# New order tables for a software-pipelined two-layer mixer kernel, and its expert weights fetched by SyncE

## The reference

```python
x = L0_attn_x                                   # [16, 512, 128] float32
xn = _layernorm(x)
s = _L0_attn_ref(xn, ...)                       # full softmax attention, 16 heads of 8
g = _silu(_L0_ffn_ref(xn, W1, W2, Wg, bg))      # top-1 of 8 experts, 128 -> 512 -> 128, gelu
x = x + s * g
xn = _layernorm(x)
s = _L1_attn_ref(xn, ...)                       # windows of 32 tokens + 64 pooled latents, gated
g = _silu(_L1_ffn_ref(xn, ...))                 # two local-attention layers (window 64, rotary,
                                                # 8 heads of 64), each with a gated feed-forward
x = x + s * g

# the expert layer
logits = xf @ Wg + bg
one_hot = jax.nn.one_hot(jnp.argmax(logits, axis=-1), e)
h = gelu(einsum('td,edh->eth', xf, W1)); y = einsum('eth,ehd->etd', h, W2)
out = einsum('etd,te->td', y, one_hot)

# one of the two layers inside _L1_ffn_ref
qkv = shift_token(x) @ wqkv; q, k = rotary_xpos(l2norm(q) * qs, l2norm(k) * ksc)
x = x + local_attention(q, k, v) @ wo
h = layernorm(shift_token(x)) * lg + lb
a, g = split(h @ w1 + b1); x = x + (a * gelu(g)) @ w2 + b2
```

## Time and profile before

| what | value |
|---|---|
| time of three runs | 3394.94, 3395.32, 3401.74 us, median 3395.32 |
| the profiled execution | 3426.32 us, of which 3424.5 us from first to last instruction |
| mean granted TensorE clock | 0.963 of full speed |
| PE busy | 3140.8 us, 92% |
| DVE busy | 2438.6 us, 71% |
| ACT busy | 2337.1 us, 68% |
| POOL busy | 1273.1 us, 37% |
| DMA | 133.97 MB, mean 39 GB/s |

### The profile page before, as it was taken

The page is one execution under the profiler, slowest core; times in us unless marked ns, Lnnn a source line. Parts: engine busy times, 40 slices in busy tenths (PEclk is TensorE's granted clock), DMA queues, the critical chain, the costliest instruction groups (busy, mean ns, idle before and its releaser), DMA issues.

```text
span 3424.5 us, 83892 instructions
## 1 busy us (share of the span) xinstructions
PE 3140.8 (92%) x34202; PEld 1900.2 (55%) x34202; DVE 2438.6 (71%) x4967; ACT 2337.1 (68%) x4800; POOL 1273.1 (37%) x817
## 2 busy tenths in 40 slices
PE   5799799999999999999999999999999999999976
PEld 5268545556564646555565646464555656464644
DVE  6621486868687877868686868778686868787643
ACT  4342277777767776777777677867777777777754
POOL 1146034433333343444333334334443333343343
PEclk8699799999999999999999999999999999999988
DMA  5346200101011111001010111110010101111000
GB/s 152 96 122 175 54 22 23 36 17 41 24 31 34 31 31 34 25 27 31 17 41 24 31 34 31 31 34 25 28 31 17 41 24 34 31 31 31 5 13 4
DMA packets 128412, 133.97 MB, mean 39 GB/s; under 512 B 18004, under 2 KB 110910, under 8 KB 128030
## 3 DMA queue, kind: packets, MB, share of 16 engines
q1 hardware_dynamic: 117872, 98.84, 11.1%
q0 software_dynamic: 10160, 29.76, 3.1%
HBM read 80.98 MB, written 30.28 MB: 32 GB/s over the span
## 4 chain that ended last, share of the span: by engine, by line
PE 53%; DVE 15%; ACT 10%; POOL 7%; issue 4%; DMA 0%; POOLq 0%; ACTq 0%; DVEq 0%
PE bank L2015 5%; PE bank L725 5%; PE bank L1453 4%; PE bank L2059 4%; PE bank L1466 4%; PE bank L2001 3%; DVE turn_f L2188 3%; PE bank L1437 3%; DVE nmax_a L1577 3%; PE bank L1982 2%; POOL turn_f L1930 2%; PE bank L1957 2%; PE bank L1991 2%; POOL y_a L1499 2%; PE bank L2065 2%
## 5 line engine op out<-in xcount | busy, mean ns | idle before, releaser
L1522 ACT ACTIVATE prob_a<-bank 128x512 f32<-128x512 f32 x1024 | 559.2, 603 | 172.0 <-PE bank L1466 165.8
L1577 DVE TENSOR_REDUCE nmax_a<-bank 128x1 f32<-128x512 f32 x768 | 499.4, 685 | 71.4 <-PE bank L1437 64.2
L1924 POOL TENSOR_TENSOR rn<-ss,minus_half 128x16 f32<-128x16 f32 x128 | 392.4, 3065 | 283.7 <-DVE ss L2183 281.8
L1947 POOL TENSOR_TENSOR rs_f<-rs_f,minus_half 128x4 f32<-128x4 f32 x32 | 32.5, 1017 | 1127.5 <-DVE rs_f L1317 1127.5
L1930 POOL TENSOR_TENSOR turn_f<-turn_f 128x512 f32<-128x512 f32 x256 | 324.8, 1289 | 169.9 <-DVE turn_f L2188 169.9
L1466 PE MATMUL bank<-Qst_a,Kst_a 74*128 74x512 bf16 x1024 | 373.4, 389 | 8.4 <-DVE nmax_a L1577 3.1
L2077 ACT ACTIVATE area<-bank 128x512 f32<-128x512 f32 x640 | 347.2, 597 | 49.6 <-PE bank L2015 41.2
L2188 DVE TENSOR_TENSOR turn_f<-area,rotf 128x1024 f32<-128x1024 f32 x256 | 306.2, 1219 | 7.2 <-POOL area L1934 6.2
L1437 PE MATMUL bank<-Kst_a,Qst_a 72*128 72x512 bf16 x768 | 302.3, 394 | 7.0 <-DMA Kst_a<-dk_a 2.4
L1453 PE MATMUL bank<-prob_a,V_a 128*9 128x512 f32 x2048 | 275.4, 610 | 26.1 <-ACT prob_a L1522 25.8
L1934 POOL TENSOR_TENSOR area<-turn_f,rn 128x1024 f32<-128x1024 f32 x128 | 254.6, 1989 | 18.6 <-POOL turn_f L1930 0.4
(11 more groups left out here) (303 smaller groups left out, 7009.6 us busy)
## 6 DMA issues: line engine op xcount, KB each, us to landing
Qst_a<-dq_a SPq DMA_DIRECT2D x192, 96.0 KB
Kst_a<-dk_a SPq DMA_DIRECT2D x192, 96.0 KB
dq_a<-prob_a SPq DMA_DIRECT2D x80, 128.0 KB
dk_a<-prob_a SPq DMA_DIRECT2D x48, 128.0 KB
ys_d<-otok_f SPq DMA_DIRECT2D x39, 128.0 KB
x_a<-in_x_in SPq DMA_DIRECT2D x16, 256.0 KB, 2.9
xn_b<-xn_n SPq DMA_DIRECT2D x16, 256.0 KB, 2.5
x_b<-x_a SPq DMA_DIRECT2D x16, 256.0 KB, 2.9
```

The lines of the kernel that those rows point to most:

```text
L1522: nc.scalar.activation(dst, bk.full(act, product)[0:rows, :], func, **kw).then_inc(a_emptied["act"], 1)
L1577: nc.vector.tensor_reduce(out=nmax_a[:, g, t, j:j + 1], in_=bk.full(dve, f)[:], op=ALU.max, axis=AX.X, negate=True).then_inc(emptied, 1)
L1924: nc.gpsimd.tensor_tensor(rn[:, t % 2], ss[:, t % 2], minus_half[:], ALU.pow).then_inc(f_root, 1)
```

## The change

Three things change.

1. All tables are replaced: `STEP`, the tables of `TIMES` and `OPEN`, and the strings of `SEATS`. The streams and their slots stay the same except for the one below. `STEP` falls from 180.102 to 178.7555.
2. `weights(j)` moves from GpSimd's stream of the opening to a new stream of SyncE, `weights_sync`. For each of the 39 blocks SyncE reads one number of `m_offs` into a register and issues a plain DMA of 128 rows of `W12`, 512 KB.
3. GpSimd no longer waits for the weights' semaphores at the opening's end, nor resets them; SyncE waits for them there.

Line numbers of the changed kernel are larger by 3 from line 924 on, and smaller by 1 between about lines 861 and 877 (the gathers L894 are L908 there).

```diff
-STEP = 180.102
+STEP = 178.7555
...
-                     (3.3175, 9.27123, 35.56572, 49.41184, 63.61356)),
+                     (4.90434, 7.96273, 8.60039, 27.32943, 51.26716)),
+            "weights": ((60, 164.1, 169, 173.9, 178.8, 183.7, 188.6, 193.5, 198.4, 203.3, 208.2, 213.1, 218,
...
+        def weights_sync(sp):
+            def weights(j):
+                first_row = sp.value_load(m_offs[0:1, j:j + 1], min_val=0, max_val=(NX - 1) * P)
+                sp.dma_start(w_ring[j % WS], W12[bass.ds(first_row, P), :]).then_inc(m_w[j % WS], 16)
+
+            yield 60
+            sp.wait_ge(m_pos, 5)
+            for j in range(WS_EARLY):
+                weights(j)
+            for j in range(WS_EARLY, NBLK):
+                yield block_slot(j - XS) + 1
+                if j == WS_EARLY:
+                    sp.wait_ge(m_sorted, 16 * 4)
+                if j >= WS:
+                    sp.wait_ge(m_y, j - WS + 1)
+                weights(j)
+            yield block_slot(NBLK) + 9.5
+            for i in range(WS):
+                sp.wait_ge(m_w[i], 16 * len(range(i, NBLK, WS)))
...
-            def weights(j):
-                nc.gpsimd.indirect_dma_start(
-                    out=w_ring[j % WS], out_offset=None, in_=W12,
-                    in_offset=bass.IndirectOffsetOnAxis(ap=m_offs[:, j:j + 1], axis=0)).then_inc(m_w[j % WS], 16)
...
-                if j >= WS_EARLY:
-                    yield block_slot(j - XS) + 1
-                    if j >= WS:
-                        pool.wait_ge(m_y, j - WS + 1)
-                    weights(j)
             yield block_slot(NBLK) + 9
-            for i in range(WS):
-                pool.wait_ge(m_w[i], 16 * len(range(i, NBLK, WS)))
```

More of the change, by code:

```diff
@@ L69 @@
             "head": ((0, 9.5, 12, 17, 29.6),
-                     (3.3175, 9.27123, 35.56572, 49.41184, 63.61356)),
+                     (4.90434, 7.96273, 8.60039, 27.32943, 51.26716)),
+            "weights": ((60, 164.1, 169, 173.9, 178.8, 183.7, 188.6, 193.5, 198.4, 203.3, 208.2, 213.1, 218,
[7 rows of a table added]
             "a": ((14, 34, 36, 56, 59, 83),
-                  (59.33356, 69.68172, 78.86345, 143.92706, 168.55117, 171.7043))},
[1 row of a table added]
         "gpsimd": {
-            "open": ((15, 18, 21, 24, 27, 30, 33, 36, 60, 147.4, 152.3, 157.2, 162.1, 164.1, 167, 169, 171.9,
[18 rows of a table removed]
+            "open": ((15, 18, 21, 24, 27, 30, 33, 36, 147.4, 152.3, 157.2, 162.1, 167, 171.9, 176.8, 181.7,
+                      186.6, 191.5, 196.4, 201.3, 206.2, 211.1, 216, 220.9, 225.8, 230.7, 235.6, 240.5, 245.4,
+                      250.3, 255.2, 260.1, 265, 269.9, 274.8, 279.7, 284.6, 289.5, 294.4, 299.3, 304.2, 309.1,
+                      314, 318.9, 323.8, 328.7, 333.6, 368.1),
+                     (-729.096, -545.2831, -221.3447, -180.39589, -180.39389, -139.05282, -36.43666, 27.16759,
+                      317.98284, 319.70985, 353.57071, 403.3216, 556.39821, 591.40663, 591.40863, 632.65447,
+                      757.3734, 995.69333, 1026.89636, 1214.81975, 1216.69564, 1351.08384, 1463.7214,
+                      1486.61817, 1514.8511, 1572.56744, 1574.60451, 1579.50739, 1603.88541, 1603.88741,
+                      1645.15018, 1645.15218, 1645.15418, 1647.91192, 1647.91392, 1647.91592, 1647.91792,
+                      1647.91992, 1647.92192, 1647.92392, 1647.92592, 1647.92792, 1647.92992, 1647.93192,
+                      1647.93392, 1647.93592, 1760.56987, 3896.46718)),
             "head": ((1, 2),
-                     (-196.74222, -195.74222))},
+                     (94.66748, 95.66748))},
         "tensor": {
@@ L252 @@
             "b": ((1.3, 2.3),
-                  (51.04818, 52.04818)),
+                  (-0.06161, 0.93839)),
             "head": ((0, 9.5, 12, 17, 29.6),
-                     (-13.55572, 22.639, 40.46466, 46.27433, 58.46796)),
+                     (-13.57442, -10.67782, 21.78004, 34.99895, 45.90457)),
             "f": ((0, 8.1, 14.2),
-                  (-41.95577, -35.8369, -30.77378)),
+                  (-129.22774, -124.54517, -67.15646)),
             "a": ((14, 34, 36, 56, 59, 83),
-                  (-103.46081, -103.45881, -97.04039, -61.756, -57.1256, -35.48245)),
+                  (-137.1201, -124.26509, -119.78701, -106.34444, -91.74503, -67.28961)),
             "finish": ((14.7, 15.7),
-                       (-48.84137, -47.84137))},
+                       (-67.57821, -66.57821))},
         "gpsimd": {
             "gate": ((0, 1),
-                     (-57.76785, -56.76785)),
+                     (-53.54468, -52.54468)),
             "b": ((0.5, 1.5),
-                  (-18.78003, -17.78003)),
+                  (-44.93433, -43.93433)),
             "head": ((1, 2),
[1 row of a table removed]
[1 row of a table added]
             "f": ((5, 6.5, 10.4, 11.9, 15.8, 17.3, 21.2, 22.7, 47, 70, 71.5, 75.4, 76.9, 80.8, 82.3, 86.2, 87.7),
[2 rows of a table removed]
[2 rows of a table added]
             "feed": ((6.8, 7.8),
-                     (-116.27669, -115.27669))},
+                     (-110.06641, -109.06641))},
         "tensor": {
@@ L378 @@
                    96.4, 97.6, 98.8, 100, 101.2, 102.4, 104.6, 108),
[10 rows of a table removed]
[10 rows of a table added]
             "feed": ((6.175, 8.3, 8.55, 9.05, 9.55),
-                     (-124.31877, -112.73997, -108.16469, -107.46893, -106.33904)),
+                     (-116.73057, -106.30141, -103.55657, -103.17137, -100.22011)),
             "finish": ((11.2, 12.2),
-                       (-98.06906, -97.06906))},
+                       (-63.94697, -62.94697))},
         "vector": {
             "gate": ((113, 113.2, 113.4),
[1 row of a table removed]
[1 row of a table added]
             "b": ((0, 0.2, 0.5, 1.5, 2.6, 3, 3.2, 3.5, 5.1, 5.2, 5.3, 5.35, 7.1, 7.2, 7.3, 7.35, 9.1, 9.2, 9.3,
@@ L425 @@
                    98.4, 99.6, 100.8, 102, 103.5, 105, 111),
[10 rows of a table removed]
[10 rows of a table added]
             "feed": ((6.55, 6.8, 7.1, 8.8, 9.3, 9.8, 10.725),
-                     (-117.34283, -116.7413, -114.69475, -107.49325, -106.47296, -104.13016, -98.61513)),
+                     (-112.76509, -111.65438, -110.77237, -103.08967, -101.79345, -99.4833, -77.78949)),
             "finish": ((13.2, 13.4, 13.6),
-                       (-85.7543, -81.99587, -49.48497))}}
+                       (-58.22573, -55.4072, -53.6288))}}
 SEATS = {
-    "a": ("254203542054321042053241510303423411324514003545035030402552035230451350243510500531031024"
-          "3120353102545202400520502353505"),
-    "b": "050234504111500034533154315435550000",
-    "head": "01221103413415325431",
-    "f": ("102451231531052304031214125341452150324254414530140041321435103131243505035235421312352412"
-          "4311012042240200"),
-    "feed": "033045214"}
+    "a": ("154203542054415324103240512302323013124514003554035030102035022530543105243150130531013001"
+          "4532011520531051023103150350342"),
+    "b": "550243503111500034533453305032530452",
+    "head": "32010321541515105430",
+    "f": ("321401341540154325031214124541423451224254512415544510520151430123510545402503420312434212"
+          "4312012042141403"),
+    "feed": "433230540"}
 B_AT = 5
@@ L900, in open_gpsimd @@
                 inverse_root(c)
-            yield 60
-            pool.wait_ge(m_pos, 5)
-            for j in range(WS_EARLY):
-                weights(j)
             for j in range(NBLK):
@@ L912, in open_gpsimd @@
                 slots(j)
-                if j >= WS_EARLY:
-                    yield block_slot(j - XS) + 1
-                    if j >= WS:
-                        pool.wait_ge(m_y, j - WS + 1)
-                    weights(j)
             yield block_slot(NBLK) + 9
-            for i in range(WS):
-                pool.wait_ge(m_w[i], 16 * len(range(i, NBLK, WS)))
             for i in range(XS):
                 pool.wait_ge(m_xs[i], 16 * ST * len(range(i, NBLK, XS)))
-            for landed in (*m_w, *m_xs):
+            for landed in m_xs:
                 pool.dma_reset(range(landed.num, landed.num + 1))
@@ L2256, in _ @@
                 def _(sp):
-                    streams((True, OPEN["sync"]["open"], open_sync(sp)), (True, OPEN["sync"]["head"], head_sync(0, sp, bk, bass.ds(0, 1), False, False)),
+                    streams((True, OPEN["sync"]["open"], open_sync(sp)), (True, OPEN["sync"]["weights"], weights_sync(sp)), (True, OPEN["sync"]["head"], head_sync(0, sp, bk, bass.ds(0, 1), False, False)),
                             (True, OPEN["sync"]["a"], a_sync(0, sp, bk)))
```

4 lines of the change are left out of this document (2 added, 2 removed), and 423 rows, old and new, of tables (OPEN, TIMES).

## The result

The changed kernel takes 3337.15 us (median of four plain runs, 3328.65 to 3341.8) against 3396.82 before; the ratio is 0.9819 with a 95% interval of 0.9804 to 0.9834. The gain is 59.7 us where 28 were forecast, and the time lies 8 us under the lower end of the range. The direction was right; the forecast gain was half of the measured one.

A forecast was written before the change was run, and what follows sets the result against it. PE was taken to bound the steady stages, leaving 8.8 us idle a stage. Rows −26 and opening −2.5 gave −28.5, so 3397.8 us profiled, scaled to 3367 us; range 3345 to 3400.

The forecast's parts named there:

- the sum of the rows: Feed-forward stages: −1.33 − 0.6 − 0.3 + 0.5 = −1.73 us a stage, over 15 stages −26 us.
- Latent scores, −1.33: Second latent score L1683: its bank wait goes with another bank, −1.33 us a stage; bounds −1.33 and 0.
- `w1`, −0.6: Fifth `w1` product no longer waits for the bank of v: −0.6 us a stage; bounds −0.7 and +0.6.
- Second q, k, v run and `xnT_b`, −0.3: Sixth product's bank wait goes, a wait for input at `xnT_b` remains: −0.3 us a stage; bounds −1.2 and +0.3.
- What stays: Waits expected unchanged: L2015 behind `hT_f` (1.28 us a stage), L1957 behind L1889 (1.10), L1453 behind `prob_a`.
- New waits, +0.5: Values L1991 waiting for the second transpose's copy, 0.4 us a stage, plus 0.1 for other new neighbours.
- POOL's gathers, 0: Four gathers in the rows move behind the fourth rotary group; worth nothing and costing nothing.
- The opening, −2.5: Row 0's stacks load ahead of two 1 MB stores, so scores start earlier: −2.5 us; bounds −3 and 0.
- Weights on SyncE, 0: 39 weight gathers leave POOL; PE bounds the blocks, so 0, at best its 11.8 us of idle time.
- Rival 2: Opening's y stores queue behind weight loads and land after more than 8.6 us: slower, 3407 us; chance 0.12.
- Rival 3: More gain: `prob_a` wait partly goes and POOL's relief gives half of 11.8 us; 3350 us, chance 0.14.

The follow-up runs named there:

- before_again: The unchanged kernel run once more for a second profile: 3399.38 us in one run, against 3395.07 before.
- rows_new: The unchanged kernel with only STEP, TIMES and SEATS of the change, its opening and weights as before: 3341.56 us against 3395.85.
- before_lat_bank: The unchanged kernel with two SEATS digits changed: second latent score on bank 4, the transpose behind it on bank 1; 3386.26 us against 3395.11.
- before_lat_chain: The unchanged kernel with three SEATS digits changed: latent scores on banks 4 and 5, the transpose behind them on bank 1; 3372.33 us against 3394.48.
- open_new: The unchanged kernel with the change's OPEN tables and weights on SyncE, its STEP, TIMES and SEATS as before: 3387.54 us against 3395.85.
- weights_pool: The changed kernel with all its tables, but the weights gathered on GpSimd as before: 3335.25 us, against 3395.85 for the unchanged kernel.
- after_gathers_back: The changed kernel with GpSimd's four gathers of y_a back between the second and third rotary groups: 3334.63 us, against 3395.07 for the unchanged kernel.
- weights_sp_only: The unchanged kernel with only the weights on SyncE and the changed tables of SyncE's opening: 3384.52 us against 3395.85.

## Why the prediction was half the size

**The step that failed is the sum of the rows, −1.73 us a stage.** Over 13 steady stages before_again takes 187.6 us a stage and rows_new 183.2. That is −4.45 a stage and −58 in all, the whole difference of the spans of these two profiles (3397.6 and 3339.8); the plain runs of rows_new gave −54.3. A stage of the unchanged kernel with its usual fall of the clock (187.41) and a usual one of the change (182.70) show how it splits. Idle time goes from 8.56 to 5.82, −2.7. The clock gives −1.3, from the rows above. PE's busy time falls by a further 0.7 that neither explains, in all but the same number of matmuls; its cause stays open.

The waits of the earlier trace rows and those of the change account for the idle part: −1.33 (latent scores), −0.70 (`w1`), −0.48 (L2015 behind `V_f`), −0.39 (values behind `mT_a`), −0.48 (L1453), −0.11 (L1957), +0.12 (`hT_f` and `xnT_b`) and +0.82 (new) make −2.55. The forecast had the first three nearly right. It missed the fourth and the fifth and put the clock at nothing.

- **The clock was missing from the sum.** The wait at the latent scores was priced at its own 1.33 us. In the unchanged kernel it also brought a fall of the clock in nine of 13 stages (before_again), −1.2 us a stage on average. The row of the twelve stages had a clock of 0.99 and I read past it.
- **Latent scores, −1.33.** Right in place and size within the full deal: no wait, and the copy still late. But before_lat_bank shows that the bad bound that I named (a wait in its place) is real, though it came at a q, k, v product and not at the two that I named: it depends on who inherits the bank. before_lat_chain got 22 us from three digits.
- **`w1`, −0.6.** The wait of 0.7 went and nothing came in its place: −0.7. With the order of the change the old bank would have cost 2.06.
- **Second q, k, v run and `xnT_b`, −0.3.** `V_f` went (−0.48), `xnT_b` stayed (0.84 against 0.75): −0.4.
- **What stays.** `hT_f` did (1.32), L1960 nearly. L1456 fell from 1.53 to 1.05, unforecast.
- **New waits, +0.5.** They were 0.8 (L724 and L1440), but in other places than the one I priced; the values got none, and lost the 0.39 that they had.
- **POOL's gathers, 0.** Right.
- **The opening, −2.5.** Too small: open_new gained 8.3. PE's wait for row 0's stacks fell by 5.1 us, from 14.14 to 9.08, not by 2 to 3. The bound of 3 us was wrong: the scores don't wait for DVE's placement chain. They started at 81.43, 2 us before its end (83.42).

```profile
81.43 1.03 PE L1428 MATMUL bank<-Kst_a,Qst_a 72*128 72x512 bf16 x2 [9.08 <-DMA Kst_a<-dk_a]
```

- **Weights on SyncE, 0.** Right: weights_pool is as fast. But the reason given, that PE's 11.8 us of idle time in the blocks were the cap, rested on an accident of one profile.
- **Rival 2 (y stores behind weights)** didn't come: the blocks kept their 3.73 us. The stores stand in one queue with the weights and land in 3.5 us at the median, the weights in 4.5 to 4.9. But the slack is smaller than the 8.6 that I took from the slow blocks of the first profile: at 3.73 us a block it is 2 × 3.73 − 0.42 = 7.0, and the longest landing in this profile was 7.0 (the trace has the landing of 20 of the 39 stores). In after_gathers_back one store took 7.4, and DVE's next copy of y waited for it, 1.8 us, once.

```profile
area<-in_W SPq DMA_DIRECT2D x25, 512.0 KB, 4.9
V_f<-in_W SPq DMA_DIRECT2D x14, 512.0 KB, 4.5
ys_d<-otok_f SPq DMA_DIRECT2D x39, 128.0 KB, 3.5
```

The rule of the Trainium skill that the prediction quotes ("DMA: Bandwidth & Descriptors", "Queues, rings and completion order") is neither refuted nor plainly shown by that. Without loads in their queue the stores land in 2.8 us (before_again), with them in 3.5 (the changed kernel, open_new) but also in 2.8 (weights_sp_only).

Rival 3 came nearest, 13 us off, for the wrong reason. It wanted its gain from a shorter chain to `prob_a`, of which 0.48 us a stage came, and from POOL's relief, which gave none.

## What to carry to other kernels

When several products share a few accumulator banks and PE's list is full, price a bank conflict by its wait and by the clock. Look at the granted clock directly behind each wait, and count a fall as the difference of PE's busy time between a stage with it and one without. Giving one product another bank only helps if the bank's next user comes later than its copy; follow the chain of heirs until one has slack, and test the chain, not the digit (22 us against 9). An order and its deal of banks belong together: this order with the old banks lost 181 us against the unchanged kernel.

A second profile of the unchanged kernel is cheap. It would have shown that a third (26.9 of 84.5 us) of the apparent saving in the first pair of profiles wasn't there.

## What the runs showed of the hardware

- In the unchanged kernel (before_again) the granted clock fell to half in nine of 13 steady stages, for 3.4 or 6.8 us, 0.2 to 2.1 us behind the end of one wait of 1.33 us; four more such waits had no fall. In the changed kernel with the conflict put back it fell in eight of 13, behind a wait of 1.55. The extra busy time was 1.3 us for 3.4 and 2.9 for 6.8, a little under half of the time spent at half clock.
- A plain DMA of 512 KB in SyncE's queue landed in 4.5 to 4.9 us at the median, and 128 KB stores between such loads in 3.5 us at the median and 7.0 at most; without the loads they took 2.8 and at most 5.8 (before_again).
- One execution of the unchanged kernel ran 22 blocks at alternately 3.84 and 5.12 us in place of 3.73, with PE's clock at full rate. The 13 other profiles of these kernels had 3.73 to 3.77 us, and its cause isn't known.
